# Both halves of the 3x3 box sums on GpSimd, with the masked weights between them

## The reference, cut to what matters

```
x = x + _L0_conv_ref(_gn(x), ...)   # 1x1 conv with weights mixed from 8 experts by a sparsemax gate
x = x + _L1_conv_ref(_gn(x), ...)   # depthwise 3x3, ReLU, prune channels, 1x1 conv, ReLU, prune
x = x + _L2_conv_ref(_gn(x), ...)   # linear attention over the 784 pixels, then a projection
x = x + _L3_conv_ref(_gn(x), 0)     # 3x3 mean of each channel, zero padded
```

## Time and profile before

| | us |
|---|---|
| median of 3 runs | 1742.29 (1740.24 to 1751.97) |
| the profiled execution, its own time | 1750.89 |
| its span, first to last instruction | 1749.1 |
| PE busy | 1608.1 (92%) |
| DVE busy | 1525.6 (87%) |
| ACT busy | 1243.9 (71%) |
| POOL busy | 420.8 (24%) |
| mean granted TensorE clock | 0.968 of full |

### The profile page before, as it was taken

One profiled execution on the slowest core, in us unless ns is written; L12 is line 12 of the kernel. 1 busy time (PEld: TensorE's weight loads), 2 busy tenths in 40 slices (PEclk: granted clock), 3 DMA queues, 4 the chain that ended last, 5 costly groups with the idle time before them and its releaser, 6 DMA issues. The chain is left out here.

```text
span 1749.1 us, 26344 instructions
## 1 busy us (share of the span) xinstructions
PE 1608.1 (92%) x8190; PEld 1138.5 (65%) x8190; DVE 1525.6 (87%) x2594; ACT 1243.9 (71%) x3240; POOL 420.8 (24%) x266
## 2 busy tenths in 40 slices
PE   4669999999999999999999999999999999999994
PEld 2237776666777666677766666766666676667773
DVE  6958799999999999989999999899999999998656
ACT  2347787777778777777777777877777787767773
POOL 1110113223211222321122232122323212232213
PEclk8759999999999999999999999999999999999997
DMA  4000011000111100011110011111001111000000
GB/s 138 19 19 19 19 37 38 26 21 29 37 37 37 37 27 20 27 37 37 37 37 19 17 37 37 37 37 37 18 18 37 37 37 37 19 19 5 33 19 37
DMA packets 21058, 55.57 MB, mean 32 GB/s; under 512 B 2322, under 2 KB 3346, under 8 KB 21011
## 3 DMA queue, kind: packets, MB, share of 16 engines
q1 hardware_dynamic: 20914, 54.98, 9.0%
q10 hardware_dynamic: 96, 0.00, 0.0%
HBM read 29.29 MB, written 25.69 MB: 31 GB/s over the span
## 5 line engine op out<-in xcount | busy, mean ns | idle before, releaser
L765 DVE SCALAR_TENSOR_TENSOR h<-xpad,dw_sb,h 128x784 f32<-128x784 f32 x512 | 502.4, 1033 | 1.2
L536 PE MATMUL tile_ps<-wqk,xn_parts 128*112 128x512 f32 x1344 | 380.4, 419 | 0.0
L536 PEld LDWEIGHTS tile_ps<-wqk,xn_parts 128*112 128x112 f32 x1344 | 222.9, 179 | 107.5 <-issue 52.8
L1195 POOL TENSOR_SCALAR xpad<-x,gn_r,gn_s 128x784 f32<-128x784 f32 x64 | 64.6, 1018 | 943.5 <-DVE gn_s L696 943.5
L1085 ACT ACTIVATE q<-tile_ps 112x256 f32<-112x256 f32 x224 | 86.1, 385 | 204.7 <-PE tile_ps L536 204.7
L578 PE MATMUL tile_ps<-k,xT 112*128 112x256 f32 x896 | 202.2, 384 | 5.1 <-ACT xT L1028 5.1
L578 PEld LDWEIGHTS tile_ps<-k,xT 112*128 112x128 f32 x896 | 172.1, 192 | 36.7 <-issue 5.8
L962 ACT ACTIVATE junk<-x 128x784 bf16<-128x784 f32 x192 | 162.3, 848 | 29.1 <-DVE x L795 14.3
L444 PE MATMUL conv_ps<-h,pw_masked 128*128 128x392 f32 x512 | 179.7, 494 | 0.7 <-issue 0.7
L566 PE MATMUL conv_ps<-x,mixed 128*128 128x392 f32 (+1 forms) x512 | 176.6, 497 | 2.2 <-ACT mixed L996 1.1
L444 PE MATMUL conv_ps<-xn_parts,w_out 128*128 128x392 f32 x768 | 153.3, 348 | 0.0
(11 more groups left out here) (138 smaller groups left out, 3074.2 us busy)
## 6 DMA issues: line engine op xcount, KB each, us to landing
x<-x SPq DMA_DIRECT2D x32, 784.0 KB, 4.4
out<-x SPq DMA_DIRECT2D x32, 784.0 KB, 3.5
expert_sb<-expert_rows SPq DMA_DIRECT2D x8, 256.0 KB, 4.9
x<-w_qk SPq DMA_DIRECT2D x1, 512.0 KB
x<-w_vT SPq DMA_DIRECT2D x1, 256.0 KB
x<-w_ln SPq DMA_DIRECT2D x1, 256.0 KB
pw_sb<-pw_wT SPq DMA_DIRECT2D x1, 256.0 KB
gmean<-group_mean SPq DMA_DIRECT2D x1, 64.0 KB, 4.2
```

The costliest lines, as they stand in the source:

```text
L536: mm = nc.tensor.matmul(bank, xn2_parts[:, u, i, m * TOK:(m + 1) * TOK], wqk[:, v, i, :], start=False, stop=(i == J - 1 and u == 1))
L765: ins = nc.vector.scalar_tensor_tensor(acc, view, scalar, acc, ALU.mult, ALU.add)
L1195: nc.gpsimd.tensor_scalar(xpad[:, j, 1:1 + H, 1:1 + W], x1[:, B.odd, j, :].rearrange("p (h w) -> p h w", w=W), gn_r[:, 1, j:j + 1], gn_s[: ...
```

## The change

VectorE's `box_sums` is taken out. GpSimd's takes the half as an argument and is called twice in a step, for half 0 ahead of `mask_weights` and for half 1 behind it. Each call waits for its own half of `x3pad` (half 0 alone for the first; before, GpSimd waited for both halves). `make_x4` on VectorE still waits for the fourth addition of each half.

```
 VectorE
-            def box_sums(F, steps):
-                for n in steps:
-                    if n == 0:
-                        dve.wait_ge(x3pad_ready.sem, x3pad_ready.at(F, 1))
-                        dve.wait_ge(setup_pool, SETUP_POOL)
-                    else:
-                        dve.wait_ge(box_step[0].sem, box_step[0].at(F, n))
-                    dst, a, b = box_operands(0, n)
-                    nc.vector.tensor_tensor(dst, a, b, ALU.add).then_inc(box_step[0].sem, 1)
...
-                if F.active:
-                    box_sums(F, range(BOX_STEPS))
 GpSimd
-            def box_sums(F):
-                pool.wait_ge(x3pad_ready.sem, x3pad_ready.at(F))
+            def box_sums(F, j):
+                pool.wait_ge(x3pad_ready.sem, x3pad_ready.at(F, j + 1))
                 for n in range(BOX_STEPS):
                     if n:
-                        pool.wait_ge(box_step[1].sem, box_step[1].at(F, n))
-                    nc.gpsimd.tensor_tensor(*box_operands(1, n), ALU.add).then_inc(box_step[1].sem, 1)
+                        pool.wait_ge(box_step[j].sem, box_step[j].at(F, n))
+                    nc.gpsimd.tensor_tensor(*box_operands(j, n), ALU.add).then_inc(box_step[j].sem, 1)
...
                 if F.active:
-                    box_sums(F)
+                    box_sums(F, 0)
                 if C_.active:
                     mask_weights(C_)
+                if F.active:
+                    box_sums(F, 1)
```

## The result

The changed kernel takes 2107.4 us (median of 4 runs, 2083.65 to 2120.65) against 1746.8 (median of 4). The slowest of the four is the profiled one; without it the ratio of the means is 1.202, with a 95% interval of 1.191 to 1.214. The profiled execution took 2120.65 us, 370 more than the one before.

A forecast was written before the change was run, and what follows sets the result against it. The step was taken to be set by a loop of group means, VectorE's list down to x2_low, then PE's work. Lateness 84, clock 32 and drain 8 made +124 on 1742.3, so 1866 us; range 1812 to 1893.

The forecast's parts named there:

- Part 1: Four additions behind x2_low taken off VectorE, 5.7 us per step: gains 0 in a level step.
- Part 2: GpSimd's earlier start holds up VectorE's small instructions through mix_w and x2_low: 3.1 us per step, 84 us in all.
- Part 3: PE's 5.1 us idle time makes its clock fall every step: 1.3 us each (between 0 and 3.2), 32 in all.
- Part 4: GpSimd's box of half 1 behind the masked weights, beside VectorE's depthwise instructions: price 0, done before make_x4.
- Part 5: In the last steps nothing covers a half, eight additions run in series on GpSimd: 8 us later together.

The follow-up runs named there:

- e1: The changed kernel with GpSimd's first box call waiting for both halves of x3pad again, so starting about 1 us later; 1752.1 us.
- e3: The changed kernel plus 12 overwritten matmuls of 512 columns on PE in the idle time ahead of the expert mixing; 1828.7 us.
- e5: The changed kernel with both GpSimd box calls behind the masked weights; 1754.9 us.
- e2: The kernel before with GpSimd's two calls swapped: half 0 stays on VectorE, half 1 goes behind the masked weights; 1687.6 us.
- e10: The changed kernel with each of the 7 thin q and k bias matmuls replaced by a full overwritten one, bias left out; 1777.1 us.
- e9: The changed kernel without the 7 thin bias matmuls in the queries and keys; 1730.1 us.
- e4: The kernel before, nothing moved, plus a 2.85 us reduction on VectorE ahead of sparsemax in the 27 steps; 1938.5 us.
- e6: The kernel before with the halves swapped: GpSimd takes half 0 and starts as early as in the change, VectorE takes half 1; 2111.2 us.
- e7: The changed kernel plus 6 overwritten matmuls of 512 columns on PE ahead of the expert mixing; 2103.0 us.
- e8: The changed kernel plus 4 matmuls behind the first convolution, lengthening the step by 0.9 us, idle time ahead of the mixing untouched; 1917.8 us.

## Why the prediction was wrong

The sign and the first half of the mechanism (GpSimd's earlier start holds up the small instructions, PE idles, the clock falls in every step) were right. The size was off by a factor of three, all of it in what follows the fall of the clock.

**Part 1, nothing gained from VectorE's missing box.** Right: e1, without that box, has a step of 51.03.

**Part 2, VectorE's list late by 3.1 us.** Measured 2.80 (75.6 us in all for the forecast 84). The gate instruction was caught, as `hmask` said. What I had wrong is the instruction behind it, the product L739, which slipped in ahead of GpSimd's third addition. So `mix_w` ended 16.9 us after the group means, not 18.6, and the last addition fell between the subtractions instead. PE's idle time was 3.34 and 0.75 us, not one piece of 5.1. My reason, that GpSimd wins each round because its next addition is ready 0.08 us after its last and VectorE's instruction comes later, was wrong: VectorE's comes 0.03 to 0.04 us after its last. Why the gate instruction lost its round all the same, though it started 0.03 us ahead, is open. Of the rule of the Trainium skill that I had cited (SBUF — State Buffer, section Who interferes with whom), the trace agrees that a `tensor_scalar` can be caught, with 1.76 us for 8 elements against 0.23 alone. That the one issued first wins can't be read off the start times: it fits the product, but not the gate instruction.

**Part 3, the clock, is the step that failed.** I took 1.3 us a step with 3.2 as the upper bound; it is 11.05 (64.85 - 51.00 - 2.80). That it would fall in every step was right. The bound was wrong, because it priced the mixing and one recovery like that of step 15 (3.4 us), and put the queries behind them at nothing; they lose 10.3 us. The trace of before held the counter-example, and I didn't price it: in step 3, in the ramp, all 42 large matmuls of the queries ran at half. The window over these queries, and over the same ones in the changed kernel:

```profile
106.19:130.30 24.11, 24.11 (x54) 13.30 (x51) 7.01 (x7) 9.23 (x34) 2.15 (x2) 0.50 0.00 1
108.13:122.76 14.63, 14.63 (x54) 8.58 (x51) 7.00 (x7) 9.22 (x34) 2.15 (x2) 0.92 0.00 1
```

The ramp is the same work in both, and it went two ways: of the ten traces with the thin matmul, five have these queries wholly at half and five have the clock back within 2.4 us of them. It is also most of why the ramp of the changed kernel is the shorter one. 27 x 11.05 less the two falls of before is 295 of the 371 us. Rows that show a thing recover once don't bound it from above.

**Part 4, half 1 behind the weights costs 0.** Right, as e1 and e3 show with the clock at full; in the changed kernel itself the slow queries hide it, since VectorE waits 9.93 us for the keys. It doesn't carry over to both halves: with all eight additions there (e5) VectorE is the bound.

**Part 5, the drain.** 7.0 us measured for 8 forecast (7.7 more in the last two steps, 0.8 less in the three ahead of them). The chain that ended last shows the eight additions in a row:

```profile
2099.46 1.50 POOL row_sums L1193
...
2106.43 1.46 POOL row_sums L1193
...
2110.35 1.84 POOL x3pad L1193
2112.23 1.76 POOLq L113
2114.01 0.98 DVE x L812
```

**The sum as it should have been:** 27 x 2.80 + 27 x 11.05 - 2.9 + 7.0 - 8.3 (ramp) = 370.

## What to carry to other kernels

Where a helper engine shares a lock with a busy one, its start is part of the busy engine's schedule: tie it behind the critical instructions, since starting it 1 us sooner cost 20% here. But not everything can go there: one half behind the masked weights gained 3.4% (e2), both gained nothing (e5). An addition of 784 elements held up an instruction of one element until it ended (1.14 us for 0.16), and a chain of small dependent instructions pays that several times. And where TensorE waits for such a chain, price the idle time and what follows it: see whether the work behind the wait has ever brought the clock back, in the ramp too, and not just how long the wait is.

## What the runs showed of the hardware

- The clock can stay at half while PE is 97% busy: 27.3 us in 27 of 27 steps, with groups of one thin bf16 matmul of 3 partitions and six large ones. With a large matmul in place of the thin one it came back after at most 2.3 us of that work, in every step (e10), and with none after at most 4.9 (e9). The Trainium skill (TensorE: Matmul & The Clock Gate, Part 1) has the clock come back once the engine is busy again; here busy wasn't enough, and the measurement decides.
- Whether the clock stays down depends on when it fell. With the bias in place, falls 2.15 to 2.4 us ahead of the queries covered all of them (82 of 82), and falls 2.8 to 3.2 us ahead did not (4 of 4); falls 5.7 to 6.6 us ahead, in e4, were over at most 1.1 us into them in 24 of 25 steps; falls that began inside the queries (two in the kernel before, three in e1, six in e3) ended after 3.4 us. Why those recover and the others don't is open: no run tells it apart.
- In the changed kernel, e6 and e7 the clock falls at the same place in nearly every level step, 1.0 to 1.1 us into the mixing, and the steps take 64.85 us. In e8, with a step 0.9 us longer, the place moves from step to step. Whether the step's length and the place of the fall hold each other was not tested.
- Six matmuls in the idle time (e7) left 2.01 and 0.67 us of it, and the clock still fell in 27 of 27 steps; twelve (e3) left 0.68 and 1.45, and it fell in 6 of 27.
